# Layer 2's state-space stage: two-bank weights, a transfer for the C rows, the gate of x beside the sines, and the inputs' sum and products in one state

## The chip, the cores and the metric

One Trainium2 chip, one of its cores. The metric is the device time of the whole kernel in microseconds, median of three runs. The kernel computes a network of four layers (sixteen stages, run one after another) on 4096 tokens of width 128. Only one of the stages, layer 2's first attention stand-in (`l2_attn_a`, a state-space scan), is touched.

## The reference, cut to what matters

```python
x_path, z = split(W_in x)                      # 256 channels each
x_path = silu(x_path)
ssm = W_x x_path                               # 16 B, 16 C, dt_in, lam_in
Bn, Cn = rmsnorm(B_raw + B_bias), rmsnorm(C_raw + C_bias)
dt  = softplus(dt_in * W_dt + b_dt);  lam = sigmoid(lam_in)
angles = cumsum(mean(dt)) * softplus(rope_freqs)
Br, Cr = rope(Bn, angles), rope(Cn, angles)
dA  = exp(A * dt)
u   = (1 - lam) * dt * dA * Bx_prev + lam * dt * Bx     # Bx = Br * x_path
u[:, 0] = dt[:, 0] * Bx[:, 0]
h   = dA * h + u ;  y = sum_n h * C            # scan over 256 positions
out = W_out ((y + D * x_path) * silu(z))
```

The kernel rewrites u: with `ahead` the term (1 - lam) dt of the following position, the previous position's part can be added before the scan, so that the scan's input is dx * B with dx = (lam dt + ahead) x, and what this puts in too early is subtracted from y once as a correction, ahead * x * (sum over n of B C). At the first position of a sequence lam dt is replaced by dt. In the code lam is (1 + tanh(lam_in / 2)) / 2.

## The kernel before, in words

The 4096 tokens are eight groups g of 512 (two sequences of 256), the 256 channels two halves i of 128 partitions, and the state 16 components n. One "state" below is one pass of the loop over n. Its steady work (class `StateScan`), by engine:

- ScalarE: `act_state`, two activations that write the decay factors `da` (exp, L2460) to PSUM, three halves deep.
- TensorE: `pe_state` spreads the row of B of component n + 2 over the partitions (L2413), then does what `between` lists for this state, then adds the two halves of h * C to y in PSUM (L2452, fp32, two passes each).
- VectorE: `dve_state`, scan of half 0 (L2522), the input u of the next component for positions 0 to 383 (L2517, dx from SBUF times the spread row from PSUM), scan of half 1, and after it what the loop of `l2_attn_a` lists.
- GpSimd: two products h * C (L2470), then the last 128 positions of u for component n + 2 (L2478), then what its `between` lists.
- SP: `sp_rows` saves B and C of a group to DRAM (L2431) and then fetches, one state after another, rows of B (L2437) and C (L2438) spread over the partitions, four deep.

Each engine runs its list in program order; the order is written out by hand, and semaphores tie the lists together. With q = g + 1 and r = g + 2, the state n of group g also prepares the next groups. Before the change, in the middle groups:

- state 0: VectorE gates y of the last group (L3316) and makes delta of q (L3254); TensorE sums B C over n (`sum_cb`); ScalarE takes the root of q.
- state 1: VectorE makes the correction (L3311) and normalises B and C of q (L3259); TensorE projects the output. State 2: TensorE sums delta; VectorE adds the output. State 3: VectorE scans delta (L3264); TensorE turns B and C.
- state 4: TensorE takes the correction; ScalarE keeps the turned rows. State 5: TensorE projects x of r; ScalarE counts the turns. State 6: TensorE adds the direct term, VectorE reduces the angles (L3268 to L3272).
- state 7: ScalarE loads a table, takes the sines of q (L3143, L3144) and the weight tanh (L3146), loads the log table again. VectorE takes statistics.
- state 9: TensorE spreads the weight over the partitions into bank 0 of `aux` (`spread_lam`); GpSimd multiplies by the sine (L3076). State 10: ScalarE gates x of r (L3124) and z; TensorE projects B, C and dt of r; GpSimd multiplies by the cosine and adds (L3080, L3084); VectorE runs `split_delta` (L3287 raw, L3290 ahead, L3292 copy).
- state 11: VectorE runs `make_dx` (L3297, L3299, L3300); TensorE projects z. States 11 to 13: GpSimd splits B into three bf16 parts (L2494, L2496). States 12 to 14: ScalarE keeps z and makes the softplus of r.
- state 14: TensorE forms the mean of squares (`spread_mean`) and moves the C rows down to partition 0 (`move_c`, L2979). State 15: VectorE multiplies B by C (`multiply_cb`, L3306).

`aux` is a PSUM tile of two banks that all these matrix products share. `size`, `lam` and others lie in a buffer that the stage borrows.

## Time and profile before

| | us |
|---|---|
| median of three runs | 4913.97 (4907.18 to 4916.18) |
| the profiled execution | 4909.32 |
| its span | 4907.4 |
| the stage's states, first scan to last | 2574.8 to about 3172 |

The times in rows are microseconds from the start of the span. PE is TensorE's matrix work and PEld its weight loads, DVE is VectorE, ACT ScalarE, POOL GpSimd. A row of the timeline gives the start, the duration, and in brackets the idle time before it and what ended that. "x2" means that two instructions are merged.

### The profile page before, as it was taken

What the parts mean: (1) busy time and instruction counts of PE and PEld (TensorE: products, weight loads), DVE (VectorE), ACT (ScalarE), POOL (GpSimd) and SP (SyncE); (2) the same over time, 40 slices, a digit from 0 to 9 for tenths busy, and PEclk for the clock granted to TensorE, in tenths of its full rate; (3) what the DMA queues carried; (4) which work ended last, traced back from release to release, by engine and by line L of the source; (5) the groups of instructions that cost most, each with busy time, mean ns of one, the idle gap of its engine ahead of it and who ended that gap; (6) DMA issues with size and microseconds to landing.
All of it is one profiled execution on the core that took longest, in us unless ns stands there. A gap on an engine that the chain in (4) does not pass through costs nothing. (4 is left out here: it accounts for less than half of the span.)

```text
span 4907.4 us, 71549 instructions
## 1 busy us (share of the span) xinstructions
PE 3529.0 (72%) x20958; PEld 2298.0 (47%) x20958; DVE 3231.1 (66%) x6387; ACT 2362.5 (48%) x4454; POOL 2120.6 (43%) x2029
## 2 busy tenths in 40 slices
PE   6867566768884548886448888749974878767686
PEld 4657355723332423333322222236653658745586
DVE  5430772069997267884349899977877766666665
ACT  3334433455651327774235455446753645544345
POOL 0046004649993435553227788721222116401254
PEclk9879777989997769997668898969986879979798
DMA  2011101145551223320223344300000001100012
GB/s 88 21 33 43 44 21 34 43 105 91 93 92 31 81 71 91 93 64 12 58 96 67 67 72 69 66 20 1 1 3 3 0 28 40 66 10 0 34 39 79
DMA packets 223543, 241.36 MB, mean 49 GB/s; under 512 B 38845, under 2 KB 170660, under 8 KB 221460
## 3 DMA queue, kind: packets, MB, share of 16 engines
q1 hardware_dynamic: 200980, 192.20, 17.0%
q0 software_dynamic: 22272, 45.66, 2.9%
q8 instruction: 137, 2.24, 0.2%
q14 instruction: 154, 1.26, 0.1%
HBM read 174.13 MB, written 62.72 MB: 48 GB/s over the span
## 5 line engine op out<-in xcount | busy, mean ns | idle before, releaser
L2452 PE MATMUL s_l_attn_a_y_ps<-XN,c_ident 128*128 128x512 f32 x1024 | 572.1, 670 | 94.6 <-POOL XN L2470 77.1
L2522 DVE TENSOR_TENSOR_SCAN s_l_attn_a_h<-s_l_attn_a_da,XN 128x512 f32<-128x512 f32 x512 | 608.2, 1210 | 22.3 <-POOL XN L2478 15.3
L2460 ACT ACTIVATE s_l_attn_a_da<-s_l_attn_a_delta,s_l_attn_a_a 128x510 f32<-128x510 f32 x512 | 346.0, 685 | 401.1 <-DVE s_l_attn_a_h L2522 398.0
L1086 POOL DMA_INDIRECT XNT<-rows_x,s_l_ffn_ffn_from_row x284 | 277.8, 978 | 464.4 <-DVE s_l_ffn_ffn_to_row L948 379.0
L960 DVE COPY s_l_ffn_ffn_xt<-s_l_ffn_ffn_turned 128x128 f32<-128x128 f32 x284 | 79.7, 291 | 555.9 <-PE s_l_ffn_ffn_turned L1161 244.3
L1091 POOL DMA_INDIRECT rows_y<-PICK,s_l_ffn_ffn_to_row x284 | 296.8, 1045 | 296.4 <-ACT PICK L1032 237.9
L1172 PE MATMUL s_l_ffn_ffn_up<-s_l_ffn_ffn_xt,s_l_ffn_ffn_own_w 128*128 128x128 f32 x2272 | 337.2, 296 | 103.6 <-DVE s_l_ffn_ffn_xt L960 100.7
L4390 DVE TENSOR_REDUCE s_l_attn_b_top<-s_l_attn_b_m_ps 128x2 f32<-128x512 f32 x512 | 330.2, 688 | 83.3 <-PE s_l_attn_b_m_ps L4096 79.4
L1182 PE MATMUL s_l_ffn_ffn_down<-down,s_l_ffn_ffn_hid 128*128 x2272 | 328.5, 291 | 75.6 <-DVE s_l_ffn_ffn_hid L974 47.7
L2452 PEld LDWEIGHTS s_l_attn_a_y_ps<-XN,c_ident 128*128 128x128 f32 x1024 | 185.0, 203 | 420.4 <-POOL XN L2470 292.2
L1172 PEld LDWEIGHTS s_l_ffn_ffn_up<-s_l_ffn_ffn_xt,s_l_ffn_ffn_own_w 128*128 128x128 f32 x2272 | 307.5, 210 | 114.6 <-DVE s_l_ffn_ffn_xt L960 111.6
L2470 POOL TENSOR_TENSOR XN<-s_l_attn_a_h,LOG 128x512 f32<-128x512 f32 x256 | 325.8, 1285 | 79.2 <-DVE s_l_attn_a_h L2522 67.4
L2470 POOL TENSOR_TENSOR XN<-s_l_attn_a_h,s_l_attn_a_more_c_rows 128x512 f32<-128x512 f32 x256 | 325.5, 1288 | 42.0 <-DVE s_l_attn_a_h L2522 29.7
L1182 PEld LDWEIGHTS s_l_ffn_ffn_down<-down,s_l_ffn_ffn_hid 128*128 128x128 f32 x2272 | 299.6, 206 | 86.0 <-issue 86.0
L4260 ACT ACTIVATE s_l_attn_b_e<-s_l_attn_b_s_ps 128x512 f32<-128x512 f32 x512 | 285.0, 604 | 42.4 <-PE s_l_attn_b_s_ps L4109 36.2
L2517 DVE TENSOR_TENSOR XN<-s_l_attn_a_dx,s_l_attn_a_spread 128x768 f32<-128x768 f32 x256 | 238.3, 931 | 27.9 <-PE s_l_attn_a_spread L2413 26.9
L1026 ACT COPY s_l_ffn_ffn_own_w<-up 128x512 f32 (+1 forms) x284 | 236.5, 834 | 39.9 <-issue 28.7
L1063 ACT ACTIVATE s_l_ffn_ffn_silu<-s_l_ffn_ffn_shifted_a 128x512 f32<-128x512 f32 x142 | 89.5, 630 | 252.0 <-DVE s_l_ffn_ffn_shifted_a L968 212.2
L3552 POOL TENSOR_TENSOR s_l_attn_b_var<-s_l_attn_b_var,s_l_attn_b_minus 128x64 f32<-128x64 f32 x8 | 84.4, 10546 | 281.7 <-DVE s_l_attn_b_var L3600 281.7
L2478 POOL TENSOR_TENSOR XN<-s_l_attn_a_dx,s_l_attn_a_b_rows 128x256 f32<-128x256 f32 x192 | 150.8, 786 | 55.2 <-DVE s_l_attn_a_dx L3299 50.1
L4124 PE MATMUL s_l_attn_b_o_ps<-s_l_attn_b_e,s_l_attn_b_vx 128*32 128x256 f32 x2048 | 165.1, 398 | 0.6
L714 POOL DMA_INDIRECT slots_x<-XN,s_l_ffn_ffn_slots x64 | 61.8, 965 | 213.6 <-DVE s_l_ffn_ffn_slots L593 182.2
(722 smaller groups left out, 8521.2 us busy)
## 6 DMA issues: line engine op xcount, KB each, us to landing
LOG<-s_l_attn_a_c_kept SPq DMA_DIRECT2D x128, 256.0 KB, 4.2
s_l_attn_a_more_c_rows<-s_l_attn_a_c_kept SPq DMA_DIRECT2D x128, 256.0 KB, 4.2
s_l_attn_a_b_rows<-s_l_attn_a_c_kept SPq DMA_DIRECT2D x192, 64.0 KB, 3.5
s_l_attn_b_qr<-s_l_attn_b_q_rows SPq DMA_DIRECT2D x64, 144.0 KB
s_l_attn_b_kr<-s_l_attn_b_k_rows SPq DMA_DIRECT2D x64, 144.0 KB
rows_x<-XN SPq DMA_DIRECT2D x8, 1024.0 KB, 3.9
XN<-rows_y SPq DMA_DIRECT2D x16, 512.0 KB, 5.1
XNT<-rows_y SPq DMA_DIRECT2D x16, 512.0 KB, 8.3
```

What stands on the lines that cost most here:

```text
L1026: nc.scalar.copy(own_w1[j % 3][:], w1[:, bass.ds(first, UP)]).then_inc(w1_ready, 1)
L1086: nc.gpsimd.indirect_dma_start(xin[j % RING], None, k.rows_x[:, :], bass.IndirectOffsetOnAxis(from_row[:, j:j + 1], 0)).then_inc(gathered[ ...
L1091: nc.gpsimd.indirect_dma_start(k.rows_y[:, :], bass.IndirectOffsetOnAxis(to_row[:, j:j + 1], 0), yout[j % RING], None).then_inc(scattered[ ...
L1172: last = nc.tensor.matmul(out[:, c % chunks, :], own_w1[j % 3][:, c * P:(c + 1) * P], xt[j % 3][:], start=True, stop=True)
L1182: last = nc.tensor.matmul(down[j % 2][:, 0:D], hid[j % 3][:, c, :], w2[:, bass.ds(first + c * D, D)], start=(c == 0), stop=(c == chunks - 1))
L2452: last = self.nc.tensor.matmul(self.y_ps[:, i, :], self.k.ident[:], self.hc[n % 2][:, i, :], start=(n == 0 and not begun), stop=(n == NST ...
L2460: self.nc.scalar.activation(self.da_half(g, n, i)[:, :, 1:], self.delta[par][:, i, :].rearrange("p (b t) -> p b t", b=BPG)[:, :, 1:], ACT. ...
L2470: self.nc.gpsimd.tensor_tensor(self.hc[n % 2][:, i, :], self.h[n % 2][:, i, :], self.c_rows[n % 4], ALU.mult).then_inc(self.hc_ready, 1)
L2517: self.nc.vector.tensor_tensor(self.u[n % 2][:, :, 0:GROUP - END], self.dx[par][:, :, 0:GROUP - END], b, ALU.mult).then_inc(self.u_ready, 1)
L2522: self.nc.vector.tensor_tensor_scan(self.h[n % 2][:, i, :], self.da_half(g, n, i).rearrange("p b t -> p (b t)"), self.u[n % 2][:, i, :], 0 ...
L4260: nc.scalar.activation(e[h][:], s_ps[BANK[n * H + h]][:], ACT.Exp, scale=HD ** -0.5).then_inc(e_ready, 1)
L4390: nc.vector.tensor_reduce(top[n % 2][:, :, h % 2, h // 2], m_ps[BANK[n * H + h]][:], AX.X, ALU.max).then_inc(max_ready, 1)
```

## The change

The weight is spread by two matrix products instead of one: bank 0 of `aux` gets (1 + tanh)/2, bank 1 (1 - tanh)/2, and VectorE multiplies delta by each. The weight's row is 1 at the first position of a sequence, where tanh is no longer written, so the copy of L3292 goes. The sum, the correction's product and dx follow at once in state 10, and dx now comes last. The C rows come to partition 0 by a transfer from the saved copy, and the product of B and C moves from state 15 to state 0 of the next group; what depends on it moves one state on. GpSimd's turn of B and C moves one state earlier, ScalarE's gate of x from state 10 to state 7.

```diff
@@ StateScan.sp_rows(self, sp, g, bc_ready, low=None)
         sp.wait_ge(self.c_saved, 16 * (g + 1))
+        if low is not None:
+            rows, rows_landed = low                    # cb, c_moved
+            sp.dma_start(rows, self.c_kept[g % 2][NST:2 * NST, :]).then_inc(rows_landed, 16)
@@ StateScan.dve_input
+        if n == 0:
+            dve.wait_ge(self.dx_made, g + 1)
@@ TensorE
             def project_ssm(q):
                 pe.wait_ge(xp_ready, q + 1)
+                since(pe, lam_read, q)
...
             def spread_lam(q):
                 pe.wait_ge(xp_ready, min(q + 2, GROUPS))
                 pe.wait_ge(lam_ready, q + 1)
-                nc.tensor.matmul(aux[:, 0, :], half_row[LAM:LAM + 2, :], lam[LAM:LAM + 2, :], start=True, stop=True).then_inc(lam_up, 1)
-            def move_c(q): ...
+                pe.wait_ge(cum_ready, q + 1)
+                pe.wait_ge(vt_ready, q + 1)
+                nc.tensor.matmul(aux[:, 0, :], half_row[LAM:LAM + 2, :], lam[LAM:LAM + 2, :], start=True, stop=True)
+                nc.tensor.matmul(aux[:, 1, :], rest_row[LAM:LAM + 2, :], lam[LAM:LAM + 2, :], start=True, stop=True).then_inc(lam_up, 1)
             def sum_cb(q):
                 pe.wait_ge(cb_ready, q + 1)
+                pe.wait_ge(z_kept, q + 1)
+                pe.wait_ge(dt_read, min(q + 2, GROUPS))
@@ TensorE between(g, n); late is 1 in group 0, else 0
-                    move_c(0)
-                if n == 2 * late:
+                if n == 1 + late:
                     sum_cb(g)
-                    if n == 2 + late:
+                    if n == 3:
                         sum_delta(q)
-                    if n == 9:
+                    if n == 8 + late:
                         spread_lam(q)
-                    if n == 14:
-                        if r < GROUPS:
-                            spread_mean(r)
-                        move_c(q)
+                    if n == 14 and r < GROUPS:
+                        spread_mean(r)
@@ GpSimd between(q, n): turn_vt (vt * sine, v * cosine) n == 9 -> 8,
   turn_bc (their sum) n == 10 -> 9; v * cosine moved from turn_bc into turn_vt
@@ ScalarE
+            def weigh(q):
+                since(act, lam_up, q)
+                nc.scalar.activation(lam[LAM:F, :].rearrange("p (b t) -> p b t", b=BPG)[:, :, 1:],
+                                     ssm[LAM:F, :].rearrange("p (b t) -> p b t", b=BPG)[:, :, 1:], ACT.Tanh, scale=0.5).then_inc(lam_ready, 1)
...
                     if n == 7 and q < GROUPS:
+                        silu_table()
+                        if r < GROUPS:
+                            gate_x(r)
+                        weigh(q)
                         sines(q)
                         log_table()
                     if n == 10:
-                        if r < GROUPS:
-                            gate_x(r)
                         gate_z(g)
                         log_table()
-                        if n == (3 if g == 0 else 0):
+                        if n == (3 if g == 0 else 1):
                             root(q)
@@ VectorE
             def split_delta(q):
                 dve.wait_ge(lam_up, q + 1)
-                dve.drain()
-                nc.vector.tensor_tensor(raw[:], delta[q % 2][:], aux[:, 0:1, :]..., ALU.mult).then_inc(lam_read, 1)
-                dve.drain()
-                ... ahead = delta - raw; raw = delta at the first position
-                dve.drain()
+                dve.wait_ge(delta_ready, q + 1)
+                since(dve, dx_ready, q)
+                nc.vector.tensor_tensor(raw[:], delta[q % 2][:], aux[:, 0:1, :].to_broadcast([P, CHH, GROUP]), ALU.mult)
+                ... ahead = delta at the next position * aux bank 1 there, then_inc(lam_read, 1)
             def make_dx(q):
-                nc.vector.tensor_tensor(dx[q % 2][:], raw[:], ahead_x, ALU.add)
-                dve.drain()
-                nc.vector.tensor_tensor(dx[q % 2][:], dx[q % 2][:], xp[q % 2][:], ALU.mult).then_inc(scan.dx_made, 1)
+                dve.wait_ge(lam_read, q + 1)
+                nc.vector.tensor_tensor(raw[:], raw[:], ahead_x, ALU.add)
+                since(dve, corrected, q)
                 nc.vector.tensor_tensor(soft, ahead_x, xp[q % 2][:], ALU.mult).then_inc(dx_ready, 1)
                 dve.drain()
+                nc.vector.tensor_tensor(dx[q % 2][:], raw[:], xp[q % 2][:], ALU.mult).then_inc(scan.dx_made, 1)
             def multiply_cb(q):
-                dve.wait_ge(c_up, q + 1)
-                nc.vector.tensor_tensor(cb, scan.rest[0:NST, :], aux[0:NST, 0, :], ALU.mult).then_inc(cb_ready, 1)
+                dve.wait_ge(c_moved, 16 * (q + 1))
+                nc.vector.tensor_tensor(cb, cb, scan.rest[0:NST, :], ALU.mult).then_inc(cb_ready, 1)
@@ VectorE, the loop; the middle groups
-  multiply_cb(q) n == 15        ->  multiply_cb(g) n == 0, ahead of make_delta(q)
-  correct(g) n == 1             ->  n == 2
-  sum_up_delta(q) n == 3        ->  n == 4
-  make_dx(q) n == 11            ->  n == 10, behind split_delta(q)
```

The two rows of weights (`half_row`, `rest_row`) move into rows of `wdt` that were unused.

## Rows read from the trace of the kernel before

**Rows 1.** The page: busy time of each engine, share of span, instructions.

```profile
PE 3529.0 (72%) x20958; PEld 2298.0 (47%) x20958; DVE 3231.1 (66%) x6387; ACT 2362.5 (48%) x4454; POOL 2120.6 (43%) x2029
```

**Rows 2.** Busy time and counts by stretch, six groups summed: us, PE, PEld, DVE, ACT, POOL.

```profile
sum 460.50, PE 367.23 PEld 130.27 DVE 429.87 ACT 235.74 POOL 376.18; mean PE 61.20 PEld 21.71 DVE 71.64 ACT 39.29 POOL 62.70
```

**Rows 3.** Waits of VectorE, 2616 to 3172 us: total us, times, longest.

```profile
DVE XN L2517 <- PE s_l_attn_a_spread L2413: 11.6, 9, 2.2
...
DVE s_l_attn_a_h L2522 <- POOL XN L2478: 10.9, 17, 1.5
```

**Rows 4.** Timeline of VectorE, one group: start us, us, what ran, [idle before].

```profile
2810.47 1.21 DVE L2522 TENSOR_TENSOR_SCAN s_l_attn_a_h<-s_l_attn_a_da,XN 128x512 f32<-128x512 f32 x1
...
2813.90 0.95 DVE L2517 TENSOR_TENSOR XN<-s_l_attn_a_dx,s_l_attn_a_spread 128x768 f32<-128x768 f32 x1 [2.22 <-PE s_l_attn_a_spread L2413]
...
2815.96 1.22 DVE L3316 TENSOR_TENSOR s_l_attn_a_y<-s_l_attn_a_y_ps,s_l_attn_a_z 128x1024 f32<-128x1024 f32 x1
...
2817.11 1.31 DVE L3254 TENSOR_TENSOR s_l_attn_a_delta<-s_l_attn_a_raw,PICK 128x1024 f32<-128x1024 f32 x1
...
2843.84 1.21 DVE L2522 TENSOR_TENSOR_SCAN s_l_attn_a_h<-s_l_attn_a_da,XN 128x512 f32<-128x512 f32 x1
...
2848.01 1.22 DVE L2522 TENSOR_TENSOR_SCAN s_l_attn_a_h<-s_l_attn_a_da,XN 128x512 f32<-128x512 f32 x1
...
2854.22 1.20 DVE L2522 TENSOR_TENSOR_SCAN s_l_attn_a_h<-s_l_attn_a_da,XN 128x512 f32<-128x512 f32 x1
...
2857.49 1.22 DVE L3287 TENSOR_TENSOR s_l_attn_a_raw<-s_l_attn_a_delta,s_l_attn_a_aux 128x1024 f32<-128x1024 f32 x1
...
2858.80 2.32 DVE L3290 TENSOR_TENSOR s_l_attn_a_ahead<-s_l_attn_a_delta,s_l_attn_a_raw 128x1020 f32<-128x1020 f32 x1
...
2861.98 1.22 DVE L2522 TENSOR_TENSOR_SCAN s_l_attn_a_h<-s_l_attn_a_da,XN 128x512 f32<-128x512 f32 x1 [0.24 <-POOL XN L2478]
...
2865.10 3.46 DVE L3297 TENSOR_TENSOR s_l_attn_a_dx<-s_l_attn_a_raw,s_l_attn_a_ahead 128x1024 f32<-128x1024 f32 x1
...
2869.92 1.93 DVE L3300 TENSOR_TENSOR LOG<-s_l_attn_a_ahead,s_l_attn_a_xp 128x1024 f32<-128x1024 f32 x1
...
2872.11 1.23 DVE L2522 TENSOR_TENSOR_SCAN s_l_attn_a_h<-s_l_attn_a_da,XN 128x512 f32<-128x512 f32 x1 [0.26 <-issue]
...
2886.66 1.22 DVE L2522 TENSOR_TENSOR_SCAN s_l_attn_a_h<-s_l_attn_a_da,XN 128x512 f32<-128x512 f32 x1 [0.28 <-POOL XN L2478]
```

**Rows 5.** Timeline of GpSimd in states 10 and 11 of that group.

```profile
2857.56 2.48 POOL L2470 TENSOR_TENSOR XN<-s_l_attn_a_h,s_l_attn_a_more_c_rows 128x512 f32<-128x512 f32 x2
...
2863.08 1.26 POOL L3084 TENSOR_TENSOR s_l_attn_a_rest<-s_l_attn_a_v,s_l_attn_a_vt 32x512 f32<-32x512 f32 x1
...
2864.30 2.48 POOL L2470 TENSOR_TENSOR XN<-s_l_attn_a_h,s_l_attn_a_more_c_rows 128x512 f32<-128x512 f32 x2
...
2866.75 0.72 POOL L2478 TENSOR_TENSOR XN<-s_l_attn_a_dx,s_l_attn_a_b_rows 128x256 f32<-128x256 f32 x1
```

**Rows 6.** Timeline of GpSimd, states 12 to 14 of the group before.

```profile
2798.68 0.73 POOL L2478 TENSOR_TENSOR XN<-s_l_attn_a_dx,PICK 128x256 f32<-128x256 f32 x1
...
2801.39 2.49 POOL L2470 TENSOR_TENSOR XN<-s_l_attn_a_h,LOG 128x512 f32<-128x512 f32 x2 [0.23 <-issue]
...
2803.84 0.73 POOL L2478 TENSOR_TENSOR XN<-s_l_attn_a_dx,PICK 128x256 f32<-128x256 f32 x1
...
2805.46 2.49 POOL L2470 TENSOR_TENSOR XN<-s_l_attn_a_h,s_l_attn_a_more_c_rows 128x512 f32<-128x512 f32 x2 [0.25 <-issue]
```

**Rows 7.** Timeline of TensorE and ScalarE, states 6 to 10.

```profile
2842.45 1.88 PE L2452 MATMUL s_l_attn_a_y_ps<-XN,c_ident 128*128 128x512 f32 x4
...
2843.95 0.63 ACT L3143 ACTIVATE s_l_attn_a_sine<-s_l_attn_a_ang 32x512 f32<-32x512 f32 x1 [3.28 <-DVE s_l_attn_a_ang L3272]
...
2847.18 1.91 ACT L2460 ACTIVATE s_l_attn_a_da<-s_l_attn_a_delta,s_l_attn_a_a 128x510 f32<-128x510 f32 x3
...
2854.36 1.02 ACT L3124 ACTIVATE s_l_attn_a_xp<-s_l_attn_a_aux 128x1024 f32<-128x1024 f32 x1
```

More of the change, by code:

```diff
@@ L2422, in da_half, with sp_rows @@
         return self.da[:, (g * (2 * NST) + 2 * n + i) % 3, :, :]
-    def sp_rows(self, sp, g, bc_ready):
+    def sp_rows(self, sp, g, bc_ready, low=None):
         sp.wait_ge(bc_ready, g + 1)
@@ L2883, in l2_attn_a @@
         w = {n: s.sb(n, shape) for n, shape in names}
-        wdt = s.sb("wdt", [DT + 1, ED])
+        wdt = s.sb("wdt", [F + 1, ED])
         loaded = s.sem("loaded")
@@ L2912, in l2_attn_a @@
         lam_ready, lam_up, lam_read, dx_ready, pick_ready = (s.sem(n) for n in ("lam_ready", "lam_up", "lam_read", "dx_ready", "pick_ready"))
-        bc_ready, c_up, cb_ready, cb_up, corrected = (s.sem(n) for n in ("bc_ready", "c_up", "cb_ready", "cb_up", "corrected"))
+        bc_ready, c_moved, cb_ready, cb_up, corrected = (s.sem(n) for n in ("bc_ready", "c_moved", "cb_ready", "cb_up", "corrected"))
         out_ready, added = s.sem("out_ready"), s.sem("added")
@@ L3068, in _ @@
             for g in range(GROUPS):
-                scan.sp_rows(sp, g, bc_ready)
+                scan.sp_rows(sp, g, bc_ready, (cb, c_moved))
         @block.gpsimd
@@ L3086, in between @@
             def between(q, n):
+                if n == 8:
+                    turn_vt(q)
                 if n == 9:
-                    turn_vt(q)
-                if n == 10:
                     turn_bc(q)
@@ L3102, in _ @@
             pool.drain()
-            nc.gpsimd.memset(half_row[:], 0.5).then_inc(cleared, 1)
+            nc.gpsimd.memset(rest_row[LAM:LAM + 2, :], 0.5)
+            pool.drain()
+            nc.gpsimd.memset(rest_row[LAM:LAM + 1, :], -0.5)
+            nc.gpsimd.memset(half_row[LAM:LAM + 2, :], 0.5).then_inc(cleared, 1)
+            pool.drain()
             pool.wait_ge(loaded, 16 * n_loads)
@@ L3159, in sizes @@
                 act.wait_ge(dt_up, q + 1)
-                since(act, dx_ready, q)
+                since(act, scan.dx_made, q)
                 since(act, delta_ready, q)
@@ L3206, in _ @@
             count_turns(0)
+            silu_table()
+            weigh(0)
             sines(0)
@@ L3285, in split_delta @@
                 dve.wait_ge(lam_up, q + 1)
-                dve.drain()
-                nc.vector.tensor_tensor(raw[:], delta[q % 2][:], aux[:, 0:1, :].to_broadcast([P, CHH, GROUP]), ALU.mult).then_inc(lam_read, 1)
-                dve.drain()
-                by_seq = [b[:].rearrange("p i (b t) -> p (i b) t", b=BPG) for b in (delta[q % 2], raw)]
-                nc.vector.tensor_tensor(ahead[:].rearrange("p i b t -> p (i b) t")[:, :, 0:SEQ - 1],
-                                        by_seq[0][:, :, 1:SEQ], by_seq[1][:, :, 1:SEQ], ALU.subtract)
@@ L3292, in split_delta @@
-                nc.vector.tensor_copy(by_seq[1][:, :, 0:1], by_seq[0][:, :, 0:1])
-                dve.drain()
+                dve.wait_ge(delta_ready, q + 1)
+                since(dve, dx_ready, q)
+                nc.vector.tensor_tensor(raw[:], delta[q % 2][:], aux[:, 0:1, :].to_broadcast([P, CHH, GROUP]), ALU.mult)
+                rest = aux[:, 1:2, :].rearrange("p a (b t) -> p a b t", b=BPG).to_broadcast([P, CHH, BPG, SEQ])
+                nc.vector.tensor_tensor(ahead[:, :, :, 0:SEQ - 1], delta[q % 2][:].rearrange("p i (b t) -> p i b t", b=BPG)[:, :, :, 1:SEQ],
+                                        rest[:, :, :, 1:SEQ], ALU.mult).then_inc(lam_read, 1)
@@ L3308, in correct @@
             def correct(q):
+                dve.wait_ge(dx_ready, q + 1)
                 dve.wait_ge(cb_up, q + 1)
@@ L3355, in _ @@
                         gate_y(g - 1)
-                    if n == late and g == 0:
-                        multiply_cb(0)
+                    if n == late:
+                        multiply_cb(g)
                     if n == late and q < GROUPS:
                         make_delta(q)
-                    if n == 1 + late:
+                    if n == (3 if g == 0 else 2):
                         correct(g)
-                        if q < GROUPS:
-                            normalise_v(q)
+                    if n == (3 if g == 0 else 1) and q < GROUPS:
+                        normalise_v(q)
                     if n == 2 and g > 0:
@@ L3368, in _ @@
                     if q < GROUPS:
-                        if n == (4 if g == 0 else 3):
+                        if n == 4:
                             sum_up_delta(q)
```

21 lines of the change are left out of this document (6 added, 15 removed).

## The prediction

> **What bounds the kernel now.** I read the page first. The busy shares of the whole span [rows 1] say little here, because the change touches one stage. The table by stretch comes next: over six middle groups of layer 2's state-space stage, 460.5 us in all or 76.75 us a group, VectorE is busy 429.9 us, 93%, and GpSimd 376.2, 82% [rows 2]. VectorE sets the length of the stage, so an edit counts only by when VectorE can start its next scan. The list of waits shows what stops it: in 556 us it waits 11.6 us for TensorE's row of B and 10.9 us for GpSimd's part of u [rows 3]. The timeline of one group then gives the place of each microsecond. I call the start of the first scan of state n Sn; the next group's start is S0'. In this group S0 is 2810.47, S7 2843.84, S8 2848.01, S10 2854.22, S11 2861.98, S12 2872.11 and S0' 2886.66 [rows 4]. A state with nothing extra takes 3.10 us (S8 to S10 is 6.21 for two). States 10 and 11, with the sum and products of inputs, take 7.76 and 10.13; states 12 to 15 take 14.55 together and not 12.4.
>
> In states 10 and 11 most of the excess is not arithmetic. The product with a PSUM operand takes 1.22 us (L3287); of the operations with two SBUF operands L3290 takes 2.32, L3297 3.46 and L3300 1.93, all on about 1024 elements [rows 4]. Beside L3290 GpSimd runs the product that ends at 2860.04; 1.1 us later L3290 ends. Beside L3297 GpSimd runs two products and the end of u up to 2867.47 [rows 5], and L3297 ends 1.1 us after that. So such an operation runs 1.1 us once GpSimd lets it in.
>
> **The change part by part.**
>
> *Weights over two banks.* The copy and the subtraction L3290 go; the second product reads PSUM, so it takes L3287's time, 1.14 from start to start, and waits for no GpSimd. What is late next is the first two-SBUF sum. TensorE issues two more matrix passes for the second bank in state 8. They lie beside three microseconds of VectorE's state and I cost them at nothing; without that cover the input of state 11 is late by up to a state's 3.1 us, most of which the queue of GpSimd described below takes up. I put 0.3 us for it.
>
> *Sum and products in state 10.* Scan two of state 10 starts at S10+1.96, the products from PSUM at +3.1 and +4.2, the sum asks at +5.5. Now GpSimd. The turn of B and C moves from states 9 and 10 to 8 and 9: two products of 1.25 us behind the end of u that finishes at S10-1.0, then the products of state 9 and its end (3.13 us a state: 2.49 for two, 0.73 for the end, less an overlap [rows 6]), then the sum of 1.26 [rows 5]. That fills GpSimd to S10+6.1, and the two products of state 10 and an end wait behind it, to +9.3 if undisturbed. If the engines take turns by instruction, the sum runs from 6.1 to 7.2, the correction's product from 8.4 to 9.5, and dx, behind a drain, from 10.7 to 11.8: S11 is S10+12.1. If VectorE loses the turn as L3297 did, it waits to +9.3 and S11 is +12.8. If it never waits, S11 is +9.1. I take 12.1, as L3290 waited for one instruction, plus the 0.3 above: 12.4.
>
> The lock is a rule too. The row: L3290 waits for one GpSimd instruction, L3297 for all that are queued [rows 4, 5]. The Trainium skill (SBUF — State Buffer, "SBUF: two separate sides") says that whichever of the two starts first holds the shared pair for its whole instruction and the other fully blocks. By it alone the sum would come out as with turns; L3297 shows that the next turn need not be VectorE's, which makes the worse end.
>
> *States 11 to 15.* Before, GpSimd's first splits of B into parts ran inside the 10.13 us of state 11. Now state 11 is 3.1 us long and GpSimd becomes the bound. A pair of split instructions costs it 1.98 us between its products (2799.41 to 2801.39), the single one 0.89 (2804.57 to 2805.46) [rows 6]. From S11: the products of state 11 and the end of 13 are done at +5.24; a pair, to +7.2; state 12, to +10.4; a pair, to +12.4; state 13, to +15.5, and S15 is +15.65; the single, state 14 and the end of u for the next group, to +19.6. So S0' is S11+19.7. The same rule gives S12+10.5 for S15 before, and VectorE there waits for GpSimd as in [rows 3]. State 10 to S0' becomes 12.4+19.7=32.1, against 2886.66-2854.22=32.44 in this group. The 4.5 us fewer of VectorE's arithmetic come to almost nothing.
>
> *C rows by a transfer, product of B and C in state 0.* Two matrix passes leave TensorE before the last y product of the group; VectorE's wait for the row of B at 2813.90, 2.22 us [rows 4], goes or shrinks. TensorE's last y product now ends with GpSimd's of state 15, at about S0'+3.4. The product of B and C has two SBUF operands and stands ahead of the sum for delta: it waits about 0.9 us, runs 0.55, then GpSimd's end of u takes 0.7, and delta 1.1. So S1 is S0'+7.8, where this group has 7.87 (gate 2815.96, delta 2817.11 to S1 at 2818.34) [rows 4]. The transfer itself is queued on SP between the save of B and C and the first rows of the next group, issued once state 11 is done; states 12 to 15 (14.55 us before) hide it, and the first row of B, needed after state 14, is issued one issue later. If it were not hidden, VectorE's product would wait in state 0.
>
> *States 1 to 6.* The correction moves from 1 to 2 and the scan of delta from 3 to 4, each 1.1 us on VectorE in either place; the count of turns on ScalarE then starts later and may hold up state 6 by 0.1. Nothing else: 25.6 against 25.5.
>
> *Gate of x beside the sines.* This is the term that I price highest. ScalarE runs it in state 7, ahead of weights and sines, and it waits for TensorE's y product of state 6, as the buffer it writes is read by the direct term of that state. That product ends at about 2844.35 [rows 7]. Now the sines start at 2843.95 after 3.28 us of waiting, the decay factors of state 8 follow at 2847.18, and VectorE's scan of state 8 starts at 2848.01, 0.14 us after the first of them [rows 4, 7]: ScalarE has no slack there. After: TensorE has both the sum over delta and the turned rows in state 3, so y of state 6 ends some 0.4 us later, S7+0.9; the gate adds 0.92 from start to start (1.02 long), then weights, sines and table as before (3.2 us), and the factors come 1.8 us later. State 7 takes 4.17+1.8=6.0. What it relieves, ScalarE in state 10, was never waited for. No gate is issued for the last two groups, so this falls in six groups. Bounds: 1.0 (the gate's length with no wait) and 3.0 (TensorE 1.2 us later still).
>
> *Removed drains, reordered waits, table loads.* A drain costs 0.1 us (the end of L3287 at 2858.71 to L3290 at 2858.80 [rows 4]); of five one stays, and one wait for VectorE's own product comes: 0.3 us, inside a stretch that GpSimd bounds. The number of table loads stays. The first group gains 1.9 us (the matrix passes that moved C before its first y) and loses up to 3.6, as its second projection now waits for VectorE's two products, 2 x 1.22 us, and one more pass; I take 1.5 lost, between -1 and +3.
>
> **Sum.** A middle group: 7.8 + 25.6 + 6.0 + 6.2 + 32.1 = 77.7 us against 76.75, so +1.0; six such make +6. The seventh, without a gate, is 75.9 against 76.2 for this group: -0.3. The last group's product in state 0 adds 0.7, the first's start 1.5. Together +7.9 us. The profiled execution took 4909.3 us (span 4907.4), so it would be 4917; the median of the three runs, 4913.97, lies 4.7 above it, which puts the forecast at 4921 to 4922.
>
> **Rivals.**
>
> *VectorE is let in at once (faster).* S11 is S10+9.1 and GpSimd's queue, never idle, gives S0' at S10+29.9: 2.2 us less in each of seven groups, 15 us, so 4906. For it: L3290, let in after one instruction. Against: GpSimd's 27 us of work from S10-1 to S0' are fixed, and three instructions of VectorE must be fitted in.
>
> *TensorE becomes the bound in states 3 to 7 (slower).* It has 16 us of passes behind the spread of state 3 in some 17 us. If they fall behind by 1.5 us (1.2 GHz for part of it), the gate starts so much later and ScalarE's chain passes it on to state 8 one for one: 6 x 1.5 = 9 us more, 4931. It decides from 0.35 us of extra delay, where the change passes the 0.2% mark. For it: two of its jobs now share state 3, and y of state 6 is the last of a queue. Against: VectorE's wait for TensorE is small now [rows 3], and state 2 loses a job.
>
> *The gate costs nothing.* If y of state 6 were early, or state 8's factors had slack, the six terms fall away: 4911. Against it stands the 0.14 us of [rows 4, 7].
>
> *Both gains at once:* 4896.
>
> **How the numbers follow.** Forecast, a cost of about 8 us: 0.42; let in at once 0.18; gate free 0.12; TensorE late 0.22; both gains 0.06. The forecast's own range is 4914 to 4930. A measurement of this kernel tells about 0.2%, 9.8 us, from no change: below 4904.1 is faster, above 4923.8 slower. The forecast gives 0.26 to same and 0.16 to slower; the first rival 0.08 to faster and 0.10 to same; the free gate 0.02 and 0.10; the slow one 0.02 to same and 0.20 to slower; the last is faster. That makes 0.16 faster, 0.48 same, 0.36 slower. The range, 4900 to 4937, takes in the first rival and the slow one with the bounds 1.0 and 3.0 of the gate.
>
> **What would show it.** State 7 at 6.0 us in the first six groups and 4.2 in the seventh, with the scan of state 8 waiting for the factors, and ScalarE waiting for TensorE before the gate. State 10 near 12 us, with the sum and both later products each held by GpSimd. VectorE waiting for GpSimd before states 14, 15 and 0', 19.7 us from S11. State 0 near 7.8 with no wait for the row of B. I am wrong if state 10 is under 10 us, if state 7 stays at 4.2, or if states 11 to 15 take 16 us.

## The result, and the profile after

The changed kernel takes 4935.22 us (median of 6 runs, 4931.64 to 4942.28), the kernel before beside it 4913.44 us (6 runs, 4903.29 to 4921.08): ratio 1.0046, 95% interval 1.0026 to 1.0066. It is 21.8 us slower. The profiled execution took 4931.64 us, its span 4929.8, against 4907.4 before.

On the page VectorE lost 24 us of work and TensorE gained 13 [rows 1]:

```profile
PE 3541.8 (72%) x20958; PEld 2316.3 (47%) x20958; DVE 3207.4 (65%) x6379; ACT 2363.3 (48%) x4454; POOL 2109.0 (43%) x2031
```

Less arithmetic on the busiest engine, and a longer run. Over the same six groups (busy time by stretch, summed) the length grew from 460.5 to 469.5 us while VectorE's busy time fell from 429.9 to 410.7, so its idle time went from 31 to 59 us [rows 2]:

```profile
sum 469.49, PE 367.84 PEld 141.57 DVE 410.74 ACT 236.06 POOL 366.66; mean PE 61.31 PEld 23.60 DVE 68.46 ACT 39.34 POOL 61.11
```

The list of VectorE's waits in this stage (total us, times, longest) names who took it. ScalarE's decay factors, at 1.1 us before, now cost 26.7; TensorE's row of B went from 11.6 to 27.8; GpSimd's part of u fell from 10.9 to 6.7 [rows 3]:

```profile
DVE XN L2522 <- PE s_l_attn_a_spread L2413: 27.8, 21, 3.1
DVE s_l_attn_a_h L2527 <- ACT s_l_attn_a_da L2463: 26.7, 18, 3.0
DVE s_l_attn_a_h L2527 <- POOL XN L2481: 6.7, 11, 1.5
```

VectorE's timeline of the group of [rows 4], in the changed kernel (start us, us, what ran, idle before). State 7 runs from 2845.66 to 2852.47, 6.8 us, and ends in a wait of 2.67 us for ScalarE; state 10 from 2858.69 to 2871.27, 12.6 us, with 3.06 us of waiting for TensorE ahead of the five operations:

```profile
2845.66 1.21 DVE L2527 TENSOR_TENSOR_SCAN s_l_attn_a_h<-s_l_attn_a_da,XN 128x512 f32<-128x512 f32 x1
...
2852.47 1.22 DVE L2527 TENSOR_TENSOR_SCAN s_l_attn_a_h<-s_l_attn_a_da,XN 128x512 f32<-128x512 f32 x1 [2.67 <-ACT s_l_attn_a_da L2463]
...
2862.95 0.95 DVE L2522 TENSOR_TENSOR XN<-s_l_attn_a_dx,s_l_attn_a_spread 128x768 f32<-128x768 f32 x1 [3.06 <-PE s_l_attn_a_spread L2413]
...
2864.95 1.19 DVE L3302 TENSOR_TENSOR s_l_attn_a_raw<-s_l_attn_a_delta,s_l_attn_a_aux 128x1024 f32<-128x1024 f32 x1
2866.06 1.21 DVE L3304 TENSOR_TENSOR s_l_attn_a_ahead<-s_l_attn_a_delta,s_l_attn_a_aux 128x1020 f32<-128x1020 f32 x1
2867.30 1.59 DVE L3310 TENSOR_TENSOR s_l_attn_a_raw<-s_l_attn_a_raw,s_l_attn_a_ahead 128x1024 f32<-128x1024 f32 x1
...
2871.27 1.22 DVE L2527 TENSOR_TENSOR_SCAN s_l_attn_a_h<-s_l_attn_a_da,XN 128x512 f32<-128x512 f32 x1
```

In the same stretch TensorE (first and last line) and ScalarE answer to [rows 7]. The y product of state 6 ends at 2847.29; the gate starts 0.09 us later, after 4.71 us of idle time (the row says "issue" and names no releaser; in the code the gate waits for this product, and in all six groups it starts 0.08 to 0.09 us behind it), and the decay factors come at 2851.66, 6.0 us after the state's first scan, where before they came 3.3 us after it:

```profile
2845.41 1.88 PE L2455 MATMUL s_l_attn_a_y_ps<-XN,c_ident 128*128 128x512 f32 x4
...
2847.38 1.02 ACT L3129 ACTIVATE s_l_attn_a_xp<-s_l_attn_a_aux 128x1024 f32<-128x1024 f32 x1 [4.71 <-issue]
...
2851.66 1.91 ACT L2463 ACTIVATE s_l_attn_a_da<-s_l_attn_a_delta,s_l_attn_a_a 128x510 f32<-128x510 f32 x3
...
2858.74 3.78 PE L2455 MATMUL s_l_attn_a_y_ps<-XN,c_ident 128*128 128x512 f32 x4
```

GpSimd's timeline [rows 5] has a hole. Its queue ends at 2867.82, and it stands idle for 4.84 us until VectorE's state 11 gives it work:

```profile
2864.65 2.48 POOL L2473 TENSOR_TENSOR XN<-s_l_attn_a_h,s_l_attn_a_more_c_rows 128x512 f32<-128x512 f32 x2
2867.10 0.72 POOL L2481 TENSOR_TENSOR XN<-s_l_attn_a_dx,s_l_attn_a_b_rows 128x256 f32<-128x256 f32 x1
2872.65 1.27 POOL L2473 TENSOR_TENSOR XN<-s_l_attn_a_h,s_l_attn_a_more_c_rows 128x512 f32<-128x512 f32 x1 [4.84 <-DVE s_l_attn_a_h L2527]
```

The scan starts of all eight groups give the lengths of the states; every kernel of this text stands in the one table. "State 0", "3 to 6" are means of groups 2 to 7, "state 7" of groups 1 to 6, "10 to 0'" of groups 1 to 7, and the stage runs from its first scan to its last gate of y. "Again" is a second profile on another chip (r_before, r_after); b_delay is the kernel before up to the end of the stage, so it counts as a third profile of it. States 1 and 2 together took 8.6 to 8.7 and states 8 and 9 took 6.2 to 6.4 in all of them.

| kernel | state 0 | 3 to 6 | state 7 | 10 and 11 | 10 to 0' | stage |
|---|---|---|---|---|---|---|
| before | 7.40 | 16.79 | 4.16 | 17.88 | 33.32 | 596.7 |
| after | 7.50 | 17.36 | 6.57 | 15.59 | 32.24 | 608.0 |
| before, again | 6.05 | 16.80 | 4.16 | 17.88 | 32.98 | 584.5 |
| after, again | 7.53 | 17.13 | 6.58 | 15.60 | 32.36 | 607.0 |
| e1_gate_back | 6.91 | 16.94 | 4.01 | 15.55 | 32.50 | 589.3 |
| e2_gate_last | 7.04 | 16.94 | 4.54 | 15.57 | 32.27 | 591.0 |
| e3_lam_early | 7.36 | 17.09 | 6.44 | 15.40 | 32.12 | 606.3 |
| e4_dx_next | 7.53 | 16.76 | 6.37 | 15.84 | 30.47 | 589.2 |
| e5_gate_dx_back | 7.94 | 16.94 | 4.00 | 15.82 | 30.42 | 578.0 |
| b_gate7 | 6.72 | 16.79 | 5.66 | 17.87 | 33.30 | 601.9 |
| b_dx10 | 6.02 | 16.79 | 4.16 | 16.50 | 33.88 | 591.7 |
| b_weights | 7.38 | 16.79 | 4.20 | 16.17 | 32.19 | 588.6 |
| b_crow | 7.39 | 17.04 | 4.16 | 17.87 | 32.57 | 593.8 |
| b_delay | 7.17 | 16.80 | 4.16 | 17.88 | 33.07 | 591.7 |

In the first pair of profiles the changed kernel is 2.7 us later when the stage begins, 11.3 us more arise in it, and 8.3 behind it, in code that the change does not touch.

### The profile page after: what moved, and what is told of

Same layout as the page of the kernel before. It is cut to its first block and busy times, and to the rows that moved or that the text cites. A ratio compares the mean times of both kernels' runs of the same rounds, so it can differ in the third digit from the quotient of the medians.

```text
span 4929.8 us, 71546 instructions
## 1 busy us (share of the span) xinstructions
PE 3541.8 (72%) x20958; PEld 2316.3 (47%) x20958; DVE 3207.4 (65%) x6379; ACT 2363.3 (48%) x4454; POOL 2109.0 (43%) x2031
## 3 DMA queue, kind: packets, MB, share of 16 engines
q1 hardware_dynamic: 201236, 192.46, 16.7%
## 5 line engine op out<-in xcount | busy, mean ns | idle before, releaser
L2455 PE MATMUL s_l_attn_a_y_ps<-XN,c_ident 128*128 128x512 f32 x1024 | 556.5, 653 | 107.6 <-POOL XN L2473 83.0
L1172 PE MATMUL s_l_ffn_ffn_up_b<-s_l_ffn_ffn_xt,s_l_ffn_ffn_own_w 128*128 128x128 f32 x1136 | 155.5, 280 | 2.1 <-issue 2.1
```

Source lines behind the costliest of these rows:

```text
L1172: last = nc.tensor.matmul(out[:, c % chunks, :], own_w1[j % 3][:, c * P:(c + 1) * P], xt[j % 3][:], start=True, stop=True)
L2455: last = self.nc.tensor.matmul(self.y_ps[:, i, :], self.k.ident[:], self.hc[n % 2][:, i, :], start=(n == 0 and not begun), stop=(n == NST ...
```

## The experiments

The kernel before had a median of 4706 to 4710 us on the chips of these runs, against 4913 in the first; each ratio is to the kernel before on the same chip. Why the first pair took some 200 us more on both sides was not looked into. The ratios and intervals are those on record; the quotient of two medians differs from them by up to 0.0013 (for b_gate7 it is 1.0031, the ratio 1.0018).

**The gate of x.** Two variants of the changed kernel: the gate back in state 10 (with the spread of the weights in state 9, as its data need it), and the gate kept in state 7 but behind weights and sines.

```
e1: n == 7:  silu_table(); weigh(q); sines(q); log_table()
    n == 10: silu_table(); gate_x(r); gate_z(g); log_table()
e2: n == 7:  silu_table(); weigh(q); sines(q); gate_x(r); log_table()
```

> The changed kernel with the gate of x back in state 10 on ScalarE, and the spread of the weights in state 9 on TensorE, as it waits for the gate (they share the PSUM banks). Theory G (the gate in state 7 is the main cost): state 7 falls from 6.2 to 6.8 us to 4.2 in the first six groups, 2.4 us each or 14 us in all, and the wait for the decay factors (2.67 us before state 8) goes. Rival T (what was lost in state 7 is only shifted: TensorE's two-bank spread, now behind the gate of state 10, holds up the input and the products): state 10 grows from 12.4 by 2 to 4 us, GpSimd's queue hides part, and the total moves by less than 5 us. G: 4921 us. T: 4930 to 4940.

Measured: 4697.28 us (10 runs), ratio 0.9979 [0.9969, 0.9989], below the kernel before itself. State 7 is 4.01 us, the stage 589.3 us, 18 less than the changed kernel's second profile (607.0, below), 15.4 of them in state 7. States 10 to 0' grew by no more than 0.14 us a group with the gate there (32.50 against 32.36), so rival T falls.

> The changed kernel with the gate of x still in state 7, but behind the weights and the sines instead of ahead of them. The gate's own length (0.92 us from start to start) stays, its wait for TensorE's y product of state 6 is then covered by the sines. Theory G: state 7 is 5.1 to 5.3 us instead of 6.2 to 6.8, so 1.0 to 1.5 us less in six groups, 6 to 9 us in all: 4927. Rival: if the table load is what the factors wait for, not the gate, nothing changes: 4935.

Measured: 4705.24 us, ratio 0.9993 [0.9983, 1.0004]; state 7 4.54 us, shorter than expected. Behind the sines the gate finds TensorE's y product done, so only part of its own length is paid. Of the 2.4 us that state 7 grew by, then, some 2 come from the place in front of the sines, where ScalarE stands and waits for TensorE.

The same part alone on the kernel before:

```
b_gate7: n == 7:  table load; gate_x(r); sines(q)        n == 10: without gate_x(r)
```

> Kernel before with one part of the change alone: the gate of x from state 10 to state 7, between the table load and the sines. Theory G (the gate delays da 8 by itself, and no slack takes it up): state 7 from 4.16 to 6.2 to 6.8 us, 7 groups by 2.2 us, the stage and the whole 14 to 16 us longer, ratio 1.003. Rival H (what that costs before state 10 comes back there, where before ScalarE's gate and VectorE's work meet): stretch of states 10 to 15 shorter by 1 to 2 us, ratio under 1.0015.

Measured: 4720.76 us (8 runs), ratio 1.0018 [1.0006, 1.0030]. State 7 grew by 1.36 us in five of the six groups (4.16 to 5.5) and by 2.2 in the first, less than expected; the stretch from state 10 kept its 33.3 us (three profiles of the kernel before have 33.0 to 33.3), so nothing is given back there and the rival falls. TensorE, ScalarE and VectorE of that run, from three timelines:

```profile
2737.67 1.88 PE L2452 MATMUL s_l_attn_a_y_ps<-XN,c_ident 128*128 128x512 f32 x4
...
2739.64 1.02 ACT L3124 ACTIVATE s_l_attn_a_xp<-s_l_attn_a_aux 128x1024 f32<-128x1024 f32 x1 [3.75 <-issue]
...
2744.59 1.22 DVE L2522 TENSOR_TENSOR_SCAN s_l_attn_a_h<-s_l_attn_a_da,XN 128x512 f32<-128x512 f32 x1 [1.38 <-ACT s_l_attn_a_da L2460]
```

The gate again starts 0.09 us behind the y product of state 6, but that one ends 0.48 us after the state's first scan (2739.07), and in the changed kernel 1.63 us after it. The other 1.1 us are TensorE's lateness, not the gate. Where it comes from, b_crow shows below.

**The spread of the weights and the products of state 10.** In the changed kernel, the spread one state earlier on TensorE; and the sum with its two products one state later on VectorE.

```
e3:  if n == 8 + late: spread_lam(q)   ->   if n == 7 + late: spread_lam(q)
e4:  n == 10: split_delta(q); make_dx(q)   ->   n == 10: split_delta(q)    n == 11: make_dx(q)
```

> The changed kernel with the two-bank spread of the weights one state earlier on TensorE, in state 7 of the middle groups, where TensorE idles while VectorE waits for the factors of state 8. In the changed kernel VectorE waits 3.06 us in state 10 for the row of B of state 11, behind the spread (four passes, about 4 us at half clock) and a slow y product. Theory Q (GpSimd's queue takes that up): the 3.06 us go, but the sum then meets GpSimd's queued products, state 10 stays between 11 and 12.1 us and state 10 to the next group's state 0 between 31.2 and 32.1: 4929 to 4935. Rival F (TensorE was the bound, VectorE is let in at once): state 10 is 9.4 us, state 10 to 0 is 29.9 us, 2.3 us less in seven groups, 16 us: 4919.

Measured: 4716.47 us, ratio 1.0015 [1.0003, 1.0027]; the wait for the row of B before the products is gone in all groups but the first, and state 10 is 12.44 us in five groups of seven all the same, somewhat above the 11 to 12.1 of theory Q. Rival F falls. The sum now asks early and waits, counted as busy: 4.09 us where it takes 1.2. VectorE in state 10 of that run:

```profile
2679.54 1.19 DVE L3302 TENSOR_TENSOR s_l_attn_a_raw<-s_l_attn_a_delta,s_l_attn_a_aux 128x1024 f32<-128x1024 f32 x1
2680.65 1.21 DVE L3304 TENSOR_TENSOR s_l_attn_a_ahead<-s_l_attn_a_delta,s_l_attn_a_aux 128x1020 f32<-128x1020 f32 x1
2681.89 4.09 DVE L3310 TENSOR_TENSOR s_l_attn_a_raw<-s_l_attn_a_raw,s_l_attn_a_ahead 128x1024 f32<-128x1024 f32 x1
2685.90 1.75 DVE L3312 TENSOR_TENSOR LOG<-s_l_attn_a_ahead,s_l_attn_a_xp 128x1024 f32<-128x1024 f32 x1
...
2688.88 1.22 DVE L2527 TENSOR_TENSOR_SCAN s_l_attn_a_h<-s_l_attn_a_da,XN 128x512 f32<-128x512 f32 x1
```

and GpSimd beside it. Its own sum runs when VectorE asks, its two products follow from 2682.42 to 2684.89, and VectorE's sum ends 1.1 us after those. The end of u behind them takes 1.70 us in place of 0.72: there VectorE got in first. Then GpSimd has nothing for 3.70 us:

```profile
2682.42 2.47 POOL L2473 TENSOR_TENSOR XN<-s_l_attn_a_h,s_l_attn_a_more_c_rows 128x512 f32<-128x512 f32 x2
2684.86 1.70 POOL L2481 TENSOR_TENSOR XN<-s_l_attn_a_dx,s_l_attn_a_b_rows 128x256 f32<-128x256 f32 x1
2690.27 1.27 POOL L2473 TENSOR_TENSOR XN<-s_l_attn_a_h,s_l_attn_a_more_c_rows 128x512 f32<-128x512 f32 x1 [3.70 <-DVE s_l_attn_a_h L2527]
```

This gives the 12.44 us its reason. The changed kernel (two profiles), e1, e2 and e3 have 35 such groups. In 34 of them GpSimd's two products ended 8.45 us behind the first scan of state 10. Where the sum then asked, be it at 5.4 or at 8.0 us behind that scan, it ended at 9.5 and state 10 took 12.43 to 12.45 us; only in the six groups where it asked at 8.6, with the end of u already running, did state 10 take 12.58 to 12.60.

> The changed kernel with the sum and the two products of inputs back in state 11, the products with the weights still in state 10. GpSimd's queue says that state 10 to the next state 0 is its 27 us of work plus what VectorE's two-SBUF operations block: Theory Q: state 10 is 7.0 to 8.5 us (with the 3.06 us wait for TensorE), state 11 is 6.4 to 8.7, depending on how long the sum waits for GpSimd's products of state 11, the splits hide beside them, and 10 to 0 comes out at 31.5 to 33: within 6 us of the changed kernel. Rival S (having all in one state is itself what helps): 10 to 0 is over 34 us and the total is 4945 or more.

Measured: 4702.74 us, ratio 0.9983 [0.9973, 0.9992]; from state 10 to 0' 30.47 us, better than any theory had it; rival S falls. The two states together are no shorter (15.84 against 15.59); what is shorter is the rest, 14.6 us against 16.7. Between the scans of state 11 GpSimd already has that state's first product, and its queue runs on while VectorE makes the sum and the products:

```profile
2756.46 0.71 POOL L2481 TENSOR_TENSOR XN<-s_l_attn_a_dx,s_l_attn_a_b_rows 128x256 f32<-128x256 f32 x1
2757.14 1.26 POOL L2473 TENSOR_TENSOR XN<-s_l_attn_a_h,s_l_attn_a_more_c_rows 128x512 f32<-128x512 f32 x1
2758.94 2.17 POOL L2473 TENSOR_TENSOR XN<-s_l_attn_a_h,s_l_attn_a_more_c_rows 128x512 f32<-128x512 f32 x1 [0.54 <-DVE s_l_attn_a_h L2527]
2761.07 1.71 POOL L2481 TENSOR_TENSOR XN<-s_l_attn_a_dx,s_l_attn_a_b_rows 128x256 f32<-128x256 f32 x1
```

The same part on the kernel before, where `make_dx(q)` goes from n == 11 to n == 10:

> Kernel before with another part alone: the sum and the products of inputs in state 10, right behind the split of delta. Theory Q (the sum waits there for the products that GpSimd has in its queue, which is not caught up by state 11): from the first scan of state 10 to the next group's first scan 33.5 to 34.5 us instead of 32.5 to 33.2, 7 to 10 us over the stage, ratio 1.0015 to 1.002. Rival T (the two states only swap their load): unchanged to within 0.3 us a group, ratio 1.000.

Measured: 4704.31 us (11 runs), ratio 0.9995 [0.9985, 1.0005]. From state 10 to 0' 33.88 us against 32.98 to 33.32 in three profiles of the kernel before: the direction of theory Q and the lower part of its range. States 10 and 11 are 1.4 us shorter and states 12 to 15 2.3 longer. The 4 to 6 us that this makes over the stage don't show in the medians.

**The weights and the C rows, each alone on the kernel before.**

```
b_weights: aux[:, 1, :] = rest_row x lam on TensorE; raw = delta * bank 0; ahead = delta * bank 1 (no difference, no copy)
b_crow:    C rows by a DMA behind the save of B and C; cb = cb * rest in state 0, its sum in 1, correction in 2; move_c gone
```

> Kernel before with the weights spread over two banks alone (two products in place of product, difference and copy with their drains; the sum and the rest stay in state 11). If VectorE's list of state 10 is the bound there: state 10 from 7.76 to 5.5 us, the next group 2.2 us earlier, 15 us over the stage, ratio 0.9968. Rival (GpSimd's splits bind from state 10 on, so the earlier end is waited for behind): the stretch from state 10 to the next group keeps 32.4 to 33 us, ratio 1.000. Rival (the second spread makes VectorE wait for TensorE as in the changed kernel): state 10 at 7.5 to 8.5 us, ratio 1.000.

Measured: 4698.42 us (11 runs), ratio 0.9982 [0.9972, 0.9991]. State 10 is 5.7 to 5.8 us in five groups of seven. In three groups the whole gain reaches the next group (10 to 0' 30.9 to 31.0 us); in the other four, 32.7 to 33.5, states 15 and 0 are long (6.1 to 6.6 and 7.8 to 8.6 us). In these four TensorE's granted clock was 0.50 over the last 4 us of state 15 and 0.50 to 0.58 over the first 3.5 us of state 0, where VectorE waited 2.1 to 2.2 us for the row of B; in two of the good ones it was 0.82 and 0.91, then 1.00, and the wait 0.2 to 0.3 us. So what is lost there goes with the clock, as in the kernel before (below). The rival on GpSimd's splits does not fit the three groups of 30.9 to 31.0 us.

> Kernel before with the C rows by a transfer alone (no product of TensorE for them, the product of B and C in state 0 with its sum over states in state 1 and the correction in state 2). Expected of it: states 0 to 2 shorter or longer by at most 1 us together, state 15 by 0.6 us shorter, ratio 0.998 to 1.000. Rival (the product of B and C waits for a transfer that starts late): state 0 longer by 1 to 2 us, ratio 1.002 to 1.003.

Measured: 4705.79 us (11 runs), ratio 1.0000 [0.9990, 1.0009]. State 0 is 7.11 us in five groups of six, state 1 3.76 (before 5.02), state 2 4.82 (3.69). State 0 of that run, VectorE:

```profile
2700.16 1.22 DVE L2525 TENSOR_TENSOR_SCAN s_l_attn_a_h<-s_l_attn_a_da,XN 128x512 f32<-128x512 f32 x1
2701.75 1.22 DVE L3311 TENSOR_TENSOR s_l_attn_a_y<-s_l_attn_a_y_ps,s_l_attn_a_z 128x1024 f32<-128x1024 f32 x1 [0.38 <-PE s_l_attn_a_y_ps L2455]
2702.90 1.31 DVE L3301 TENSOR_TENSOR s_l_attn_a_vt<-s_l_attn_a_vt,s_l_attn_a_rest 16x512 f32<-16x512 f32 x1
2704.14 1.21 DVE L3249 TENSOR_TENSOR s_l_attn_a_delta<-s_l_attn_a_raw,PICK 128x1024 f32<-128x1024 f32 x1
```

The product of B and C follows the gate of y without idle time, so the transfer isn't late and the rival falls by its mechanism. The state is longer nonetheless at an equal clock, as the table below shows. This part also makes TensorE late. Its sum over states now stands in state 1. Over the first 5 us from the first scan of that state the granted clock was 0.77 to 0.97 in groups two to six, and the projection of the output took 2.7 to 3.8 us (in all three profiles of the kernel before, 1.00 and 1.95 us). The y product of state 6 then ends 1.2 to 1.6 us behind the first scan of state 7 in the first six groups. In the group of the next line that scan starts at 2730.66, so it is 1.24 us, against 0.5 in the kernel before:

```profile
2730.02 1.88 PE L2455 MATMUL s_l_attn_a_y_ps<-XN,c_ident 128*128 128x512 f32 x4
```

In b_crow nobody waits for that, as no gate stands in state 7; in the changed kernel the gate waits for it. The ratios of the four parts alone come to 0.9995 together, the whole change to 1.0016 (below): the parts are not independent. GpSimd's turn of B and C, one state earlier, was not run by itself.

**Both costly parts back, and what lies behind the stage.**

```
e5:      e1 and e4 together: gate of x in state 10, spread_lam in state 9, make_dx in state 11
b_delay: kernel before + 12 x (drain; copy 128x1020 from PSUM) on VectorE behind the last group
```

> Changed kernel with two parts undone at once: the gate of x goes back to state 10 and the sum with its products of inputs to state 11. Theory G (the gate in state 7 holds da 8 back by its own 1.05 us and the group's sines, and nothing gives that back) and theory Q (VectorE's sum waits for GpSimd's whole queue in state 10, a queue that has run shorter by state 11) are two separate costs: state 7 comes down from 6.4 to about 4.1 us and the stretch from the first scan of state 10 to that of the next group from 32.3 to 30.2 to 31.2 us, so a group falls by 3.5 us, the stage by 26 to 30 us to 578 to 582, ratio to the kernel before 0.994 to 0.996. Rival (the two share one slack, so that the second gives nothing beside the first): stage 588 to 591, ratio 0.998.

Measured: 4690.48 us (6 runs), ratio 0.9959 [0.9946, 0.9972]: faster than both kernels, by 19 us than the one before and by 27 us than the changed one beside it. The stage is 578.0 us, 29.0 less than the changed kernel's there; back from it one by one the gate gave 17.7 and the products 17.8. Their sum is 35.5; the 6.5 us by which e5 falls short of it lie in state 0 (7.94 us here, 6.91 in e1, 7.53 in e4), where the clock decides (below). Where the two parts act, both gains are there in full: state 7 fell by 15.4 us over six groups, as in e1, and states 10 to 0' by 13.5 over seven (13.2 in e4). They are two separate costs.

> The changed kernel once more, on the same chip as its variants. If the 8 us of the profiled difference that arise after the stage, in code that the change does not touch, are its doing, the ratio is again about 1.0046; if they are chance of one pair of profiles, the ratio is that of the stage alone, 14 of 4909 us, 1.003, and the second trace shows a stage of 606 to 610 us and a difference after it other than 8.

> The kernel before, unchanged, for its trace on this chip: stage near 596.7 us as in the first profile, group lengths within 1 us of it, state 7 at 4.2 us, state 10 at 7.8 and state 11 at 10.1.

Measured: the changed kernel 4717.80 us (12 runs), ratio 1.0016 [1.0005, 1.0027]; the kernel before, in its one profiled run, 4703.13. The traces of the two have 4.5 us more ahead of the stage, 22.5 us more in it and 12.4 us less behind it. So the 8.3 us behind the stage in the first pair are not the change's doing. The stretch behind the stage, the same code in all kernels, took 1633 to 1647 us in eleven profiles of these chips.

What the stage costs is less sure than one pair of traces makes it look. The expectation for the kernel before missed: its stage is 584.5 us and not 596.7, with 8.1 us of the difference in state 0 and 2.4 in states 10 to 0', and a third profile (b_delay) has 591.7. The changed kernel has 608.0 and 607.0, which is 10 to 24 us more. By stretch (busy times, then granted clock, DMA share and GB/s), the first 3.5 us of state 0, first in r_before:

```profile
2699.10:2702.60 3.50, 3.50 (x10) 1.33 (x9) 3.30 (x5) 0.92 (x2) 3.50 (x4) 1.00 0.56 100
```

and in the first profile of the same kernel, in the group of [rows 4]:

```profile
2810.50:2814.00 3.50, 3.50 (x6) 1.48 (x5) 1.28 (x3) 0.69 (x1) 1.71 (x3) 0.50 0.63 111
```

Of the two levels, 1.00 is 2.4 GHz and 0.50 is 1.2 GHz. All groups two to seven of five profiles, sorted by the granted clock in this stretch:

| kernel | clock | groups | VectorE's wait for the row of B | state 0 |
|---|---|---|---|---|
| before (three profiles) | 1.00 | 6 | 0.20 | 5.86 to 6.23 |
| | 0.56 to 0.62 | 7 | 0.99 to 1.37 | 6.66 to 7.03 |
| | 0.50 to 0.51 | 5 | 2.22 | 7.87 |
| changed (two profiles) | 1.00 | 9 | none | 7.10 to 7.11, one 6.29 |
| | 0.65 | 1 | 1.82 | 8.08 |
| | 0.50 | 2 | 2.53 to 2.54 | 9.48 to 9.49 |

At an equal clock the change makes state 0 longer, by about 1.1 us at 1.00 and 1.6 us at 0.50. In the first pair this didn't show, as the kernel before had no group at 1.00 and the changed kernel five of six. b_crow, with its 7.11 us at 1.00, says that it comes with the C rows' part.

> Kernel before with a pure delay on VectorE behind the stage's last group: 12 copies of 128x1020 from PSUM, with drains, some 14 to 15 us, whose result nobody needs. Theory shift (a later arrival at the expert stages costs more than itself, since transfers and granted clock fall otherwise there): the whole is 20 to 24 us longer. Rival (a delay is carried through one for one): 13 to 16 us longer. Second rival (cover behind the stage takes part of it): under 10.

Measured: 4724.07 us (10 runs), ratio 1.0027 [1.0015, 1.0039], 14.3 us above the kernel before. The copies took 15.45 us. By the medians a delay is carried through about one for one (by the interval it may be 7 to 18 us), so the first theory falls:

```profile
3069.08 15.45 DVE L3384 COPY s_l_attn_a_ahead<-s_l_attn_a_y_ps 128x1020 f32<-128x1020 f32 x12
```

## Why the prediction came out as it did

The time, 4935.22, lies within the range of 4900 to 4937 and 14 us above the forecast; slower had a chance of 0.36 and same 0.48. That it lies near the upper bound is in part chance: in the profiles 8.3 us arose behind the stage, and on another chip the medians are 8.0 us apart. Two of its terms came out by luck. Taken by its own steps:

*The gate of x.* The mechanism is as written: ScalarE waits for the y product of state 6, the sines and the factors follow, state 8 waits. The size was low: state 7 takes 6.57 and not 6.0 us in the first six groups, and 4.06 in the seventh. The term that was off is "y of state 6 ends at S7+0.9"; it ends at S7+1.0 in the first group, S7+1.22 in two and S7+1.63 in three (before, +0.49 in the group of [rows 4]), because TensorE's passes follow one another without a gap from 2827.06 to 2847.29 in the group shown (before, it still waited 0.60 us for VectorE at 2833.36). The cause that I named, two jobs in state 3, can't be all of it: b_crow has one job there and is as late (1.24 us in most groups), with the sum over states in state 1 and a lower clock behind its first scan. The clock has its part: in the three groups with 1.63 the projection of the output in state 1 took 3.78 us, before 1.95. How much the order and the clock have each was not separated. In these three groups the lateness is about half of what the rival on TensorE in states 3 to 7 said. States 3 to 6, priced at next to nothing, took 17.36 against 16.79 us, with short waits for TensorE's rows of B (0.5 to 1.0 us a group). That is 6 x 0.57 = 3.4 us for state 7 and as much again for the others. e1 shows what the gate's place costs: 15.4 us in state 7, 18 of the stage.

*Weights on TensorE, hidden.* Right, though not as argued. In the group shown the wait for the row of B is 3.06 us, the very bound that I named, as TensorE had the half clock there (granted clock 0.50 from 2855 to 2859, 2.07 and 1.91 us for the two spreads, 3.78 for a y product of 1.88). e3 took that wait away and state 10 stayed at 12.44 us, so it does lie in GpSimd's shadow.

*Sum and products in state 10.* Forecast 12.4, measured 12.44 in most groups. The number was hit by luck; neither of the two cases that I worked out is what happened. With turns by instruction the sum should have run from S10+6.1 to +7.2, with each later product held by GpSimd. In e3, without TensorE's wait, it asked at +5.4, lost the turn to both products of h and C, got in at +8.45 ahead of the end of u, and ended at +9.5, 2.3 us later than forecast. The correction's product then waited 0.5 us for the end of u, and dx for nothing, where I had priced a wait for each. The worse end (in at +9.3, behind the end of u) did not happen either. The Trainium skill (SBUF — State Buffer, "SBUF: two separate sides") says that the engine that starts first holds the shared pair for its whole instruction. The trace of e3 agrees: GpSimd's two products ran before the waiting sum did, and the end of u took 1.70 us while the sum ran. Why VectorE did not get in between the two products but did behind the second stays open.

*States 11 to 15.* Right: S11 to S0' forecast 19.7 us, measured 19.69 to 19.99 in the seven groups. But I called the lost 4.5 us of VectorE's arithmetic "almost nothing" as if the splits alone were the reason. e4 shows the step behind it: GpSimd bounds this stretch, and five operations in one state leave it idle (3.7 us in five groups, 4.84 in two) because its next input is a scan behind them. With two of them in state 10 and three in state 11 it is idle for 0.54 us in the group shown, and 1.9 us a group come out.

*State 0.* Forecast 7.8, measured 7.11 in five of the six groups and 7.50 in the mean. The comparison was worse than the number: I took the group of [rows 4] for the kernel before, whose 7.87 us belong to a granted clock of 0.50. Its mean is 7.40, and 6.05 and 7.17 in other profiles. That the state kept its length in the first pair was luck: at an equal clock the change costs 1.1 us or more there, and I had put that at nothing. In the same way 32.44 us for states 10 to 0' was the lowest of its groups, of mean 33.32: this stretch gained 1.1 us a group and not 0.3, which hid 5 us of what state 7 and its neighbours cost beyond the forecast.

*The sum.* Forecast +7.9 us; measured 14.0 at the end of the stage: 9.0 in the groups two to seven (forecast 4.7: five with the gate at 1.0 less 0.3 for the seventh), 2.2 in the last (0.7), 0.1 in the first and 2.7 ahead of its first scan (2.5 together).

*Behind the stage.* I forecast nothing there, and the traces do not speak against it: the 8.3 us of the first pair turn into 12.4 less in the second. Which part of those later stages varies by 14 us between executions stays open; so does how much of the gap between the ratios 1.0046 and 1.0016, whose intervals only just touch, is the chip's.

*The rivals.* "Let in at once" is falsified by e3, "gate free" by e1, and "both gains" with them. "TensorE late" happened to about half of its 1.5 us in three groups and to less in the others, in part by the half clock that it named.

## What to carry to other kernels

Before work is moved earlier, look at what the engine that bounds the next stretch is waiting for: the sum and products that stand ahead of the scan which feeds GpSimd cost 1.9 us a group more in state 10 than in state 11. An operation that must wait for another engine belongs behind those that others wait for: ahead of the sines the gate cost 2.4 us a group, behind them 0.4. And a baseline is not one group: take all groups of two or more profiles, and compare groups of an equal granted clock.
